# Masks in half rows, work moved to ScalarE, and half of the second attention's queries transposed in mid-step

## The chip, the core and the metric

The kernel runs on one core of a Trainium2 chip: TensorE (matmuls, with its weight loads shown as PEld), VectorE (DVE), ScalarE (ACT), GpSimd (POOL) and SyncE (SP), which start DMAs and wait for each other on semaphores. The metric is the device time of one execution in microseconds, the median of several.

## The reference

The input is 16 sequences of 256 tokens with 128 features. Layer 0 is: half a mixture of experts, attention, half a mixture; layer 1 the same with other formulas.

```python
x = x + 0.5 * _L0_ffn_ref(_layernorm(x), ...)   # top 2 of 8 experts, capacity, exact gelu, 128-512-128
x = x + _L0_attn_ref(_layernorm(x), ...)        # 16 heads of 8, rotation, distance decay, causal mask
x = x + 0.5 * _L0_ffn_ref(_layernorm(x), ...)
x = x + 0.5 * _L1_ffn_ref(_layernorm(x), ...)   # top 2 of 8 experts, silu(a) * g, biases
x = x + _L1_attn_ref(_layernorm(x), ...)        # q, k, v with bias, each head normed, no mask
x = x + 0.5 * _L1_ffn_ref(_layernorm(x), ...)
```

The attention core, for a batch b and a head h of 8 features, with all pairs of 256 queries and 256 keys:

```python
scores = einsum(q, k) / sqrt(8)                 # layer 0: + decay, -inf above the diagonal
out = softmax(scores) @ v
out = out @ Wo
```

## The kernel before

The program runs ten stages one after another, with a barrier between them: setup, token stage t0, experts e0, causal attention a0, experts e1, token stage t1, experts e2, full attention a1, experts e3, token stage t2. Tokens stay in SBUF in `x_res`. A token stage goes over 16 batches of 256 tokens: it adds the experts' gated results (`Combine`, L224), norms the rows (`Norm`, L292), chooses two experts (`Route`) and scatters each token's row twice into slots in memory, by four indirect DMAs per batch that GpSimd issues (`pool_scatter`, L545). The routed rows, with their row number as a 129th word, are written twice side by side by VectorE (`dve_rows`, L339).

An attention stage (`attention_stage`, L783) does the same around the attention, as a pipeline written out by hand: each engine has its own `causal_step(s, u)` or `full_step(s, u)`, and these lists set the order on that engine. In step s TensorE computes scores for batch s and exponent inputs for batch s-1; the combining and norm are done for batch s+3, the projection for s+2, the operands for s+1, the division, output projection and residual for s-2, and the routing for s-3.

Each batch has 16 units of two heads. `scores` (L1693) fills one of two PSUM tiles `psS`, from 54 rows of bf16 parts at partitions 0 or 64 (r = unit mod 2); VectorE takes the row maximum (`unit_max`, L1098); unit n+2 waits for the maximum of unit n. When all maxima of a batch are there, VectorE writes them, negated and split in two, into the operand `ext` (`max_rows`, L1105); TensorE transposes the queries again with them (`queries`, L1703, two halves t, into `psA` and `psD`), and VectorE and ScalarE copy the halves to `QM` (`queries_out`, L1112 and L1484). Then `e` (L1734) computes score minus maximum, transposed, in 56 rows, ScalarE takes the exponential (`unit_exp`, L1500), and `unit_v` (L1742) multiplies by the values (fp32, column tiles of 32). `weighted_out` copies the sums from PSUM: half on ScalarE (L1491), half on VectorE (L1126). In the causal stage each unit opens with a mask product of 128 rows and 256 columns, identity times mask, for scores (L1689) and for exponents (L1730).

The projection's result is copied by ScalarE with the token's norm as scale in the causal stage (L1439), and by VectorE with norm and bias in the full one (L1068). GpSimd in the full stage scales heads, takes the two rests of the bf16 splitting (`left_of_a`, `left_of_b`), scatters batch s-3, and computes both norms' reciprocal roots. `Combine.dve_gate` (L257) copies the gates of a batch, and a one-element copy (L276) marks that they were used.

## Time and profile before

| | us |
|---|---|
| median of three runs | 1839.45 (1837.21 to 1840.55) |
| profiled execution | 1845.23, its span 1843.4 |
| TensorE, weight loads busy | 1337.0 (73%), 867.6 (47%) |
| VectorE busy | 1118.2 (61%) |
| ScalarE busy | 702.6 (38%) |
| GpSimd busy | 876.2 (48%) |

Busy shares are means over ten stages that differ; matmuls overlap, so a busy TensorE is not one at its peak. a0 lies at about 250 to 690 us, a1 at about 1135 to 1645 us. In names `<-` means output from inputs, `x` a count, and what stands in brackets is how long the engine was idle before and who released it; "issue" means that nothing in the profile released it.

### The profile page before, as it was taken

To read this page: it belongs to the slowest core of one execution; us is meant where nothing else is said; L and a number is where in the kernel's file an instruction comes from. 1 tells how busy PE (TensorE), PEld (TensorE's weight loads), DVE (VectorE), ACT (ScalarE), POOL (GpSimd) and SP (SyncE) were. 2 spreads that over 40 slices of the span, in tenths; PEclk is the share of its full clock that TensorE was granted. 3 is DMA by queue.
4 is the path that set the end of the run, shared out by engine and by line. 5 is a ranking of instruction groups with operands and counts; after the bars stand their busy time and mean duration, and the time that the engine had idled before them with its cause. 6 is when DMAs were issued, how large, how long until landed. Compare 5 with 4: busy or idle time off the path is not lost. (4 is left out here: it accounts for less than half of the span.)

```text
span 1843.4 us, 34564 instructions
## 1 busy us (share of the span) xinstructions
PE 1337.0 (73%) x10630; PEld 867.6 (47%) x10630; DVE 1118.2 (61%) x4074; ACT 702.6 (38%) x1370; POOL 876.2 (48%) x1148
## 2 busy tenths in 40 slices
PE   3359938998888884994328883687878888838880
PEld 2249923444444433994216772333334334427770
DVE  6622246877887743224874444797888787644446
ACT  1112225766666641221012221475565566502220
POOL 5745535345545322554774562535454444225560
PEclk9999967999999975997559996698898787959995
DMA  9312216544000001222316672000000000026664
GB/s 286 111 48 70 71 49 152 126 99 92 22 21 13 13 13 30 73 71 76 89 44 193 198 203 78 12 13 24 18 17 20 14 12 7 14 68 190 201 181 143
DMA packets 105370, 146.31 MB, mean 79 GB/s; under 512 B 14192, under 2 KB 84336, under 8 KB 105264
## 3 DMA queue, kind: packets, MB, share of 16 engines
q1 hardware_dynamic: 85824, 107.07, 21.9%
q0 software_dynamic: 17408, 35.82, 5.7%
q10 hardware_dynamic: 2032, 2.10, 0.4%
q8 instruction: 56, 0.92, 0.2%
q14 instruction: 50, 0.41, 0.1%
HBM read 80.53 MB, written 64.40 MB: 79 GB/s over the span
## 5 line engine op out<-in xcount | busy, mean ns | idle before, releaser
L1505 ACT ACTIVATE a_PT<-a_psE 128x512 f32<-128x512 f32 (+1 forms) x512 | 273.5, 545 | 223.0 <-PE a_psE L1738 209.3
L1102 DVE TENSOR_REDUCE a_mx<-a_psS 128x2 f32<-128x512 f32 (+1 forms) x512 | 311.8, 617 | 40.6 <-PE a_psS L1697 31.4
L1697 PE MATMUL a_psS<-a_KT,a_QT 54*128 54x256 bf16 (+1 forms) x1024 | 189.6, 284 | 38.5 <-DVE a_mx L1102 34.6
L1738 PE MATMUL a_psE<-a_QM,a_KT 56*128 56x256 bf16 (+1 forms) x1024 | 194.1, 279 | 13.7 <-issue 6.6
L2166 PE MATMUL e_psH<-e_rowsT,e_w 128*128 128x256 f32 x640 | 164.4, 402 | 38.9 <-DVE e_rowsT L2206 24.8
L1762 PE MATMUL a_psV<-a_PT,a_vx 128*32 128x256 f32 (+1 forms) x2048 | 174.3, 393 | 16.4 <-ACT a_PT L1505 14.5
L2245 POOL DMA_INDIRECT slots_y<-e_y,e_ids x160 | 155.3, 970 | 46.6 <-issue 24.6
L2197 ACT ACTIVATE e_sg<-e_psH,e_w 128x256 f32<-128x256 f32 x160 | 67.1, 470 | 230.0 <-PE e_psH L2166 165.9
L2166 PEld LDWEIGHTS e_psH<-e_rowsT,e_w 128*128 128x128 f32 x640 | 120.3, 198 | 61.5 <-DVE e_rowsT L2206 25.1
L2080 POOL DMA_INDIRECT slots_y<-e_y,e_ids x128 | 124.2, 970 | 48.3 <-POOL e_ids L2078 28.8
L2044 ACT ACTIVATE e_hT<-e_psH 128x1024 f32<-128x1024 f32 x64 | 65.5, 1024 | 184.2 <-PE e_psH L2016 184.2
L2016 PE MATMUL e_psH<-e_rowsT,kept_w 128*128 128x256 f32 x512 | 128.7, 397 | 2.2 <-DVE e_rowsT L2061 2.2
L1697 PEld LDWEIGHTS a_psS<-a_KT,a_QT 54*128 54x128 bf16 x1024 | 56.4, 97 | 152.0 <-issue 69.8
L2025 PE MATMUL e_psY<-kept_w,e_hT 128*128 128x128 f32 x1024 | 124.6, 275 | 0.0
L2025 PEld LDWEIGHTS e_psY<-kept_w,e_hT 128*128 128x128 f32 x1024 | 119.6, 192 | 0.1
L2206 DVE COPY e_rowsT<-e_psT 128x256 f32<-128x256 f32 x80 | 33.9, 424 | 132.0 <-PE e_psT L2159 73.6
L2016 PEld LDWEIGHTS e_psH<-e_rowsT,kept_w 128*128 128x128 f32 x512 | 96.7, 199 | 15.3 <-DVE e_rowsT L2061 3.8
L1015 POOL TENSOR_TENSOR a_left<-a_left,a_ext 128x512 f32<-128x512 f32 x32 | 37.7, 1177 | 127.2 <-DVE a_ext L1091 127.2
L2175 PE MATMUL e_psY<-e_w,e_hT 128*128 128x128 f32 x640 | 87.6, 281 | 3.4 <-DVE e_hT L2211 3.4
L2061 DVE COPY e_rowsT<-e_psT 128x256 f32<-128x256 f32 x64 | 27.2, 425 | 102.6 <-PE e_psT L2008 102.6
L2175 PEld LDWEIGHTS e_psY<-e_w,e_hT 128*128 128x128 f32 x640 | 80.9, 198 | 3.9 <-DVE e_hT L2211 3.8
L1762 PEld LDWEIGHTS a_psV<-a_PT,a_vx 128*32 128x32 f32 x2048 | 44.6, 111 | 78.8 <-issue 40.4
(347 smaller groups left out, 2944.4 us busy)
## 6 DMA issues: line engine op xcount, KB each, us to landing
e_w<-in_pack SPq DMA_DIRECT2D x80, 450.0 KB
slots_x<-tail SPq DMA_DIRECT2D x8, 2193.0 KB
e_rows<-slots_x SPq DMA_DIRECT2D x80, 129.0 KB
e_rows<-spans_x SPq DMA_DIRECT2D x64, 129.0 KB
a_got<-slots_y SPq DMA_DIRECT2D x32, 256.0 KB
t_got<-slots_y SPq DMA_DIRECT2D x32, 256.0 KB
slots_y<-e_y,e_ids POOLq DMA_INDIRECT x288
spans_x<-tail SPq DMA_DIRECT2D x4, 1032.0 KB, 10.2
```

What stands on the lines that cost most here:

```text
L1102: nc.vector.tensor_reduce(mx[u][:, t, 4 * g + r:4 * g + r + 3:2], psS[c % 2][:, :, 0:cols], AX, ALU.max).then_inc(s_max, 1)
L1505: nc.scalar.activation(PT[:, c % 4, :, q0:SEQ], psE[c % 2][:, :, q0:SEQ], ACT.Exp).then_inc(s_e, 1)
L1697: ins = nc.tensor.matmul(psS[c % 2][:, hh, 0:cols], QT[u][64 * r:64 * r + MAXR, k, t * P:(t + 1) * P], KT[u][64 * r:64 * r + MAXR, k, 0:co ...
L1738: ins = nc.tensor.matmul(psE[c % 2][:, hh, q0:SEQ], KT[u][64 * r:64 * r + MAXR + 2, k, kt * P:(kt + 1) * P], QM[64 * r:64 * r + MAXR + 2, ...
L1762: last = nc.tensor.matmul(psV[g // 2][32 * quad:32 * quad + 32, g % 2, q0:SEQ], vx[u][:, kt, head, :], PT[:, c % 4, hh, q0:SEQ], start=(kt ...
L2016: last = nc.tensor.matmul(psH[j % 2][:, c, :], w[:, j // KEPT_TILES, c * P:(c + 1) * P], rowsT[:, j % 2, :], start=True, stop=True)
L2025: last = nc.tensor.matmul(psY[j % 2][:, s * D:(s + 1) * D], hT[:, j % 2, c, s * P:(s + 1) * P], w[:, j // KEPT_TILES, UP + c * D:UP + (c + ...
L2080: pool.indirect_dma_start(slots_out, bass.IndirectOffsetOnAxis(ap=ids[:, j % U, s:s + 1].bitcast(U32), axis=0), y[:, j % U, s, :], None).t ...
L2166: last = nc.tensor.matmul(psH[u % 2][:, c, :], w[:, u, c * P:(c + 1) * P], rowsT[:, u % 2, :], start=True, stop=True)
L2175: last = nc.tensor.matmul(psY[u % 2][:, s * D:(s + 1) * D], hT[:, u % 2, c, s * P:(s + 1) * P], w[:, u, DOWN0 + c * D:DOWN0 + (c + 1) * D] ...
L2197: ins = nc.scalar.activation(sg[:, u % 2, c, :], psH[u % 2][:, c, :], ACT.Silu, bias=w[:, u, B1 + c:B1 + c + 1])
L2245: pool.indirect_dma_start(slots_out, bass.IndirectOffsetOnAxis(ap=ids[:, u, s:s + 1].bitcast(U32), axis=0), y[:, u, s, :], None).then_inc( ...
```

## The change

- Masks: each 128-row mask product becomes two of 64 rows (`scores_mask`, `e_mask`), in the row half that the unit's data uses; the first covers 256 columns, the second only the 128 in which its rows mask anything. They are issued alternately for the two units in work.
- ScalarE takes over: the second half of the weighted values (at the start of the next step); in the full stage both projection copies (the norm's scale is put on the tokens before they are transposed, the bias comes from an added product of a constant matrix with the bias), and the routed rows as x * rstd + shift, shift computed by GpSimd; the gates' copy; in the other stages the second copy of the routed rows. The marker copy becomes a bare semaphore increment.
- `QM` has two buffers, and `max_rows` runs once per half. In the full stage the first half of the queries is transposed at n == 9 of the batch's own step and copied after maximum 11; operands come one unit earlier; the scatter is of batch s-4 and stands between the two rests; VectorE's list is reordered.

```diff
+    def act_gate(self, act, b, u):
+
+        wait(act, self.s_added, b - 1)
+        self.nc.scalar.copy(self.gate[:, u, :].rearrange("p (t k) -> p t k", t=TPB),
+                            self.keep.gates[:, bass.ds(b * TPB, TPB), :]).then_inc(self.s_gate, 1)
...
-            nc.vector.tensor_copy(self.used[:, u:u + 1], self.gate[:, u, 0:1]).then_inc(self.s_added, 1)
+            dve.sem_inc(self.s_added, 1)
...
+            if self.to_scatter:
+                nc.vector.tensor_scalar(self.less[:, u, :], self.mv[:, u, :, 0], -1.0, None,
+                                        ALU.mult).then_inc(self.s_less, 1)
...
-            self.out[:, w, t, :, 0:D], x.to_broadcast([P, TOPK, D]),
+            self.out[:, w, t, 0, 0:D].unsqueeze(1), self.keep.x[:, bass.ds(b * TPB + t, 1), :],
...
+    def act_second(self, act, b, w):
...
+        self.nc.scalar.copy(self.out[:, w, :, 1, 0:D], self.out[:, w, :, 0, 0:D]).then_inc(self.s_second, 1)
...
+        self.nc.gpsimd.tensor_tensor(self.shift[:, u, :], self.less[:, u, :], self.rstd[:, u, :],
+                                     ALU.mult).then_inc(self.s_shift, 1)
...
+    def act_rows(self, act, b, u, w):
+
+        act.wait_ge(self.s_shift, b + 1)
+        act.wait_ge(self.s_ids, b + 1)
+        for t in range(TPB):
+            ins = self.nc.scalar.activation(
+                self.out[:, w, t, :, 0:D], self.keep.x[:, bass.ds(b * TPB + t, 1), :].to_broadcast([P, TOPK, D]),
+                ACT.Identity, scale=self.rstd[:, u, t:t + 1], bias=self.shift[:, u, t:t + 1])
+        ins.then_inc(self.s_out, 1)
...
+        wait(pool, self.norm.s_out if by_act else self.norm.s_second, b + 1)
...
+                if has(s - 4):
+                    route.pool_scatter(pool, chain, s - 4, u, True)
                 if has(s + 1):
                     left_of_b(s + 1, v)
-                if has(s - 3):
-                    route.pool_scatter(pool, chain, s - 3, v)
...
+                    route.norm.pool_shift(pool, s - 2, u)
...
+            if not causal:
+                route.pool_scatter(pool, chain, BATCHES - 1, 1, True)
...
-                dst = [ext[u][:, :, 0, :, MAXR + n] for n in range(2)]
-                link(nc.vector.tensor_scalar(dst[0], mx[u][:, :, :], -1.0, None, ALU.mult))
-                nc.vector.scalar_tensor_tensor(out=dst[1], in0=mx[u][:, :, :], scalar=-1.0,
+            def max_rows(b, u, t):
+                dve.wait_ge(s_max, UNITS * b + 8 * (t + 1))
+                dst = [ext[u][:, t, 0, :, MAXR + n] for n in range(2)]
...
+                wait(dve, s_E, UNITS * (b - 1))
+                nc.vector.tensor_copy(QM[u][:, :, 0:P].bitcast(U32),
                                       psA[:, :].bitcast(U32).rearrange("p (k q) -> p k q", k=8)).then_inc(s_QM[0], 1)
...
-                rows(0)
+                if has(s + 3):
+                    dve.wait_ge(comb.s_gate, s + 4)
+                add(0, 0)
                 maxima(1, 2)
-                rows(1)
+                add(0, 1)
                 maxima(2, 3)
                 if has(s - 2):
                     divide(s - 2, 0)
+                add(1, 0)
                 maxima(3, 4)
-                if has(s + 3):
-                    comb.dve_gate(dve, link, s + 3, v)
-                add(0, 0)
-                maxima(4, 5)
                 if has(s + 1):
                     split_a(s + 1, v)
+                maxima(4, 5)
+                add(1, 1)
+                maxima(5, 6)
                 if has(s - 2):
                     divide(s - 2, 1)
-                maxima(5, 6)
-                add(0, 1)
-                add(1, 0)
+                do(stats, 0)
                 maxima(6, 7)
-                if has(s + 2):
-                    project_out(s + 2, u, 0)
+                if has(s + 1):
+                    split_b(s + 1, v)
+                do(stats, 1)
                 maxima(7, 8)
                 for n in range(5):
                     do(choose, n)
+                    do(stats, n + 2)
                 maxima(8, 9)
-                if has(s + 1):
-                    split_b(s + 1, v)
-                add(1, 1)
+                if has(s):
+                    max_rows(s, u, 0)
                 maxima(9, 10)
-                if has(s + 2):
-                    project_out(s + 2, u, 1)
                 do(number, 0)
                 do(number, 1)
                 maxima(10, 11)
-                if has(s - 2):
-                    route.dve_ids(dve, s - 2, u)
+                if has(s + 1):
+                    split_c(s + 1, v)
                 do(number, 2)
                 maxima(11, 12)
+                if has(s):
+                    queries_out(s, u)
                 do(number, 3)
-                if has(s + 1):
-                    split_c(s + 1, v)
-                do(number, 4)
+                if has(s + 2):
+                    head_var(s + 2, u)
                 maxima(12, 13)
                 if has(s - 2):
                     residual(s - 2)
+                do(number, 4)
                 maxima(13, 14)
                 if has(s - 2):
-                    link.sync()
-                    dve.sem_inc(s_xr, 1)
-                do(stats, 0)
-                if has(s + 2):
-                    head_var(s + 2, u)
-                do(stats, 1)
+                    route_stats(s - 2, u)
...
+                    max_rows(s, u, 1)
                 if has(s + 1):
                     last_operand_out(s + 1, v)
-                if has(s):
-                    queries_out(s)
-                if has(s - 1):
-                    weighted_out(s - 1, v)
                 link.restart()
             step = causal_step if causal else full_step
...
+            def scaled_tokens_out(b, u):
+                act.wait_ge(norm.s_rstd, b + 1)
+                wait(act, s_xaT_ps, b - 1)
+                for t in range(TPB):
+                    ins = nc.scalar.activation(xs[:, u, t, :].unsqueeze(1), keep.x[:, bass.ds(b * TPB + t, 1), :],
+                                               ACT.Identity, scale=norm.rstd[:, u, t:t + 1])
+                ins.then_inc(s_xs, 1)
...
+            def scaled_project_out(b, u, t):
+                act.wait_ge(s_proj, TPB * b + t + 1)
+                if t == 0:
+                    wait(act, s_v, b - 1)
+                nc.scalar.copy(pr[:, u, t, :], psA[:, 0:QKV]).then_inc(s_pr, 1)
...
+            def weighted_out(b, u, n):
+
+                act.wait_ge(s_V, UNITS * b + 8 * (n + 1))
+                nc.scalar.copy(oT[u][:, 2 * n:2 * n + 2, :], psV[n][:, :, :]).then_inc(s_oT[n], 1)
...
+                exps(0, 1)
+                if has(s - 3):
+                    route.norm.act_rows(act, s - 3, v, v)
+                exps(1, 2)
                 if has(s + 2):
                     tiles_out(s + 2)
-                exps(3, 5)
+                exps(2, 4)
                 if has(s - 3):
                     route.act_T(act, s - 3, v, psT)
+                exps(4, 5)
+                if has(s + 2):
+                    scaled_project_out(s + 2, u, 0)
                 exps(5, 6)
-                exps(6, 7)
                 if has(s + 1):
                     copies_of_a(s + 1, v)
-                exps(7, 8)
+                exps(6, 8)
+                if has(s + 2):
+                    scaled_project_out(s + 2, u, 1)
                 if has(s - 2):
                     divided_out(s - 2)
                 exps(8, 9)
+                if has(s + 1):
+                    copies_of_b(s + 1, v)
                 exps(9, 10)
                 if has(s - 1):
-                    weighted_out(s - 1, v)
-                if has(s + 1):
-                    copies_of_b(s + 1, v)
-                exps(10, 11)
+                    weighted_out(s - 1, v, 0)
                 if has(s + 2):
                     squares(s + 2, u)
+                exps(10, 11)
+                if has(s + 3):
+                    scaled_tokens_out(s + 3, v)
                 exps(11, 12)
-                if has(s + 3):
-                    tokens_out(s + 3, v)
-                exps(12, 14)
+                if has(s + 4):
+                    comb.act_gate(act, s + 4, u)
+                exps(12, 13)
                 if has(s + 1):
                     operands_out(s + 1, v, 0)
-                exps(14, 15)
+                if has(s + 2):
+                    heads_log(s + 2)
+                exps(13, 14)
+                if has(s + 2):
+                    heads_rsqrt(s + 2)
                 if has(s + 1):
                     operands_out(s + 1, v, 1)
-                if has(s + 2):
-                    heads_log(s + 2)
-                exps(15, 16)
-                if has(s + 2):
-                    heads_rsqrt(s + 2)
+                exps(14, 16)
                 if has(s + 1):
                     operands_out(s + 1, v, 2)
...
+                if not causal:
+                    nc.tensor.matmul(psA[:, 0:QKV], mean_of[:, :], par[:, BI0:BI0 + QKV],
+                                     start=True, stop=False, skip_group_check=True)
                 nc.tensor.matmul(psA[:, 0:QKV], xaT[:, t * P:(t + 1) * P], wqkv[:, :],
-                                 start=True, stop=True).then_inc(s_proj, 1)
+                                 start=causal, stop=True, skip_group_check=True).then_inc(s_proj, 1)
...
-                    nc.tensor.matmul(psS[c % 2][:, :, t * P:(t + 1) * P], identb[:, :],
-                                     masks[:, 0, :].unsqueeze(1).to_broadcast([P, 2, P]), start=True, stop=False,
-                                     skip_group_check=True)
+                    scores_mask(c, 0)
+
+            def scores_mask(c, i):
+
+                t, g, r = unit_b(c)
+                rows, lo = slice(64 * r, 64 * r + 64), 64 * i
+                nc.tensor.matmul(psS[c % 2][:, :, t * P + lo:(t + 1) * P], half_ident[rows, i, :],
+                                 masks[rows, 0, i, lo:P].unsqueeze(1).to_broadcast([64, 2, P - lo]),
+                                 start=(i == 0), stop=False, skip_group_check=True)
             def scores(u, c, hh):
                 t, g, r = unit_b(c)
...
+                rows, hi = slice(64 * r, 64 * r + 64), 64 * (i + 1)
+                nc.tensor.matmul(psE[c % 2][:, :, kt * P:kt * P + hi], half_ident[rows, i, :],
+                                 masks[rows, 1, i, 0:hi].unsqueeze(1).to_broadcast([64, 2, hi]),
+                                 start=(i == 1), stop=False, skip_group_check=True)
...
+                    if has(s) and n < UNITS - 2:
+                        scores_mask(n + 2, 1)
+                    if has(s - 1) and n < UNITS - 1:
+                        e_mask(n + 1, 0)
                     for hh in range(2):
...
-                    queries(s - 1, v, 0)
...
+                    if n == 9 and has(s):
+                        queries(s, u, 0)
...
+                    if n == 11 and has(s + 1):
+                        operands(s + 1, v, 0)
                     if n == 12 and has(s + 1):
-                        operands(s + 1, v, 0)
+                        operands(s + 1, v, 1)
                     if n == 13 and has(s + 1):
-                        operands(s + 1, v, 1)
-                    if n == 14 and has(s + 1):
                         operands(s + 1, v, 2)
                 if has(s + 1):
...
+    half = P // 2
+    twice = [np.tile(m[i * half:(i + 1) * half], (2, 1)) for m in (above * MASKED, above.T * MASKED, np.eye(P))
+             for i in range(2)]
+    return np.concatenate([ang, pos] + twice, 1).astype(np.float32)
```

## Rows read from the trace of the kernel before

**Rows 1.** Busy by stretch: length, PE (x), PEld, DVE, ACT, POOL, granted clock, DMA share, GB/s.
```profile
308.20:665.00 356.80, 319.65 (x3509) 161.97 (x3510) 275.94 (x941) 229.75 (x490) 159.42 (x197) 0.99 0.24 56
1188.40:1599.20 410.80, 339.27 (x3058) 158.02 (x3059) 331.66 (x956) 249.83 (x488) 183.37 (x231) 0.85 0.05 16
```

**Rows 2.** One line (VectorE's query copies): duration min/median/max, first and last start.
```profile
L1116 DVE COPY a_QM<-a_psA x16: 680/692/693, 308.2 to 665.0; 128x512 uint32<-128x512 uint32 x16
...
L1116 DVE COPY a_QM<-a_psA x16: 681/691/693, 1188.4 to 1599.2; 128x512 uint32<-128x512 uint32 x16
```

**Rows 3.** Waits, TensorE's loads, 308.2 to 665: us in total, times, longest.
```profile
PEld a_psS L1697 <- issue: 44.3, 207, 0.4
PEld a_psS L1689 <- DVE a_mx L1102: 21.4, 51, 1.0
```

**Rows 4.** Timeline, first attention, one unit: start, duration, instruction [idle before it].
```profile
442.00 0.28 PE L1689 MATMUL a_psS<-a_masks,a_identb 128*128 128x256 bf16 x1
...
442.12 0.27 PE L1730 MATMUL a_psE<-a_masks,a_identb 128*128 128x256 bf16 x1
...
442.32 0.28 PE L1697 MATMUL a_psS<-a_KT,a_QT 54*128 54x256 bf16 x1
442.32 0.28 PE L1738 MATMUL a_psE<-a_QM,a_KT 56*128 56x256 bf16 x1
...
442.64 0.43 PE L1762 MATMUL a_psV<-a_PT,a_vx 128*32 128x128 f32 x8
```

**Rows 5.** Waits, second attention, 1188.4 to 1599.2, of three engines.
```profile
PEld a_psS L1697 <- DVE a_mx L1102: 49.8, 75, 1.4
...
DVE a_QM L1116 <- PE a_psA L1720: 30.7, 15, 3.2
...
ACT a_PT L1505 <- PE a_psE L1738: 101.4, 115, 2.8
```

**Rows 6.** Timeline of VectorE, second attention, a step's end.
```profile
1311.79 0.69 DVE L1102 TENSOR_REDUCE a_mx<-a_psS 128x2 f32<-128x512 f32 x1
...
1316.38 0.69 DVE L1116 COPY a_QM<-a_psA 128x512 uint32<-128x512 uint32 x1 [1.98 <-PE a_psA L1720]
...
1317.59 0.68 DVE L1102 TENSOR_REDUCE a_mx<-a_psS 128x2 f32<-128x512 f32 x1
```

**Rows 7.** VectorE's groups, second attention, last row first attention: busy us, mean ns | idle.
```profile
L1073 DVE SCALAR_TENSOR_TENSOR a_pr<-a_psA,a_attn_rstd,a_par 128x384 f32<-128x384 f32 x26 | 15.9, 613 | 5.1 <-PE a_psA L1642 4.8
L344 DVE TENSOR_SCALAR a_route_out<-x_res,a_route_mv,a_route_rstd 128x256 f32 x16 | 15.9, 995 | 0.0
...
L344 DVE TENSOR_SCALAR a_route_out<-x_res,a_route_mv,a_route_rstd 128x256 f32<-128x256 f32 x10 | 8.0, 803 | 0.0
...
L276 DVE COPY a_used<-a_gate_b 128x1 f32<-128x1 f32 x12 | 1.8, 154 | 0.4
...
L344 DVE TENSOR_SCALAR a_route_out<-x_res,a_route_mv,a_route_rstd 128x256 f32 x16 | 5.8, 409 | 0.0
```

**Rows 8.** ScalarE's groups: from the first attention, then from the second.
```profile
L1442 ACT ACTIVATE a_pr<-a_psA,a_attn_rstd 128x384 f32<-128x384 f32 x26 | 15.1, 580 | 6.0 <-PE a_psA L1642 4.5
...
L1494 ACT COPY a_oT<-a_psV 128x512 f32<-128x512 f32 x15 | 8.8, 585 | 0.0
```

**Rows 9.** Page, section 5, a ScalarE group with a bias from memory.
```profile
L2197 ACT ACTIVATE e_sg<-e_psH,e_w 128x256 f32<-128x256 f32 x160 | 67.1, 470 | 230.0 <-PE e_psH L2166 165.9
```

**Rows 10.** Timeline, second attention: projections in its steady part, and at its start.
```profile
1297.88 0.91 PE L1642 MATMUL a_psA<-a_wqkv,a_xaT 128*128 128x384 f32 x2
...
1145.49 1.65 PE L1642 MATMUL a_psA<-a_wqkv,a_xaT 128*128 128x384 f32 x2 [0.46 <-ACT a_xaT L1434]
```

**Rows 11.** Timeline of GpSimd, second attention: the first residue, and a scatter.
```profile
1296.08 1.16 POOL L1011 TENSOR_TENSOR a_left<-a_qk,a_ext 128x512 f32<-128x512 f32 x1 [2.90 <-DVE a_ext L1087]
...
1311.39 0.96 POOL L551 DMA_INDIRECT slots_x<-a_route_out,a_rows  x1 [0.30 <-issue]
```

**Rows 12.** Timeline of GpSimd, second token stage.
```profile
923.31 0.22 POOL L549 TENSOR_TENSOR t_rows<-t_rows,no_rows 128x4 int32<-128x4 int32 x1 [0.24 <-DVE t_rows L539]
```

150 lines of the change are left out of this document (81 added, 69 removed).

## Prediction

> **What bounds the kernel now.** I read the busy times by stretch first [rows 1]. The two attention stages take most of the span: their steady parts are 356.8 and 410.8 us, each 15 steps long (from the first to the last of 16 copies of one kind [rows 2]), so a step takes 23.8 us in the first attention and 27.4 us in the second. Per step VectorE is busy 275.94/15 = 18.4 us and 331.66/15 = 22.1 us, ScalarE 15.3 and 16.7 us. No engine is full; each step is a chain of 16 units, handed from TensorE (scores) to VectorE (row maximum) and, one batch behind, from TensorE to ScalarE (exponential) and back, and TensorE issues all of it in one order. So I read next who waits for whom.
>
> In the **first attention** [rows 3] TensorE's mask loads wait 21.4 us in all for maxima (1.4 a step), but its score loads show 44.3 us with "issue" as the reason, 207 pieces of about 0.2 us: there it waits for nobody, the array is finishing. One unit in close order [rows 4] shows what that is: the mask product for scores starts at 442.00, the one for the exponentials at 442.12, the data products only at 442.32, the next work at 442.64. Same shape follows same shape after 0.12 us; from a 128-row mask to 54- or 56-row data takes 0.20 us, and the two rounds of data leave the same 0.32 = 0.12 + 0.20 us until the next shape. TensorE paces the middle of this step, VectorE comes close behind.
>
> In the **second attention** [rows 5] there are no masks. TensorE's score loads wait 49.8 us for maxima (3.3 us a step); VectorE's largest wait is 30.7 us (2.05 a step) for the transposed queries at the end of the step. VectorE paces the middle, and between the last maximum of a step (ends 1312.48) and the first of the next (1317.59) lie 5.1 us [rows 6]: two maximum rows, a copy of keys, 1.98 us of waiting for the transposed queries, their copy (0.69), the copy of weighted values. The granted clock is 0.99 in the first and 0.85 in the second stage [rows 1]; 0.85 is a mix of the two levels, 2.4 GHz for 70% of the time and 1.2 GHz for 30%.
>
> **The change, part by part.** *Masks.* The 128-row product of 256 columns becomes two 64-row products of 256 and 128 columns, in the rows of the array which its unit uses; the other unit's mask has the other rows. The trace shows data products of the two units starting within 0.01 us of each other [rows 4], but no 64-row mask. If the halves overlap likewise, a unit runs 0.12 + 0.06 (128 columns, half of 0.12), then data at once: data starts 0.18 instead of 0.32 us after the mask, 0.14 saved, and 0.08 more where the next unit follows without another shape between. If they do not overlap, 0.12 + 0.12 + 0.06 + 0.06 = 0.36 us, 0.04 lost. Bounds -0.04 and +0.22; I take 0.17 a unit, since the data products do overlap: 15 x 0.17 = 2.6 us of TensorE a step. A page of the Trainium skill, TensorE: Matmul & The Clock Gate (Part 3, Measured speedup vs the span model), has four row tiles gaining 3.07 times instead of 4. Scaled that way my 0.18 would be 0.23 us, by an estimate from that page 0.8 us a step and 12 us of the total less; no row here shows packed masks.
>
> *VectorE, second attention* [rows 7], per step: both projection outputs go (15.9/13 = 1.22), both routed-row writes ((15.9 + 8.0)/13 = 1.84), the copy of weighted values (0.69, as the copy of the same size [rows 6]), gate copy and the marker copy behind it (0.15 for the marker, 0.2 taken for the gates). Sum 4.1. Added: the maximum rows are done in two halves (two operations more, each at least as long as the marker's 0.154 [rows 7]; between 0.3 and 0.55, I take 0.4) and one small negation, 0.17. Net -3.5: 22.1 becomes 18.6.
>
> *ScalarE, second attention.* Two projection copies of 384 columns: 0.585 is the price of 512 columns, 0.58 that of 384 with a scale from memory [rows 8], so less than both, I take 0.48 and 0.1 for a scale: 2 x 0.48; weighted values 0.585; tokens scaled in two pieces instead of one copy, about +0.33; routed rows 2 x 0.47 to 0.57 (nearest: 128x256 with a bias, 0.47 [rows 9]), 1.05; gates about 0.2 (bounds 0.15 to 0.4). Together +3.1: 16.7 becomes 19.8. The first attention gets weighted values, the second copy of routed rows (half the columns of the weighted values, 0.4) and gates: +1.2, to 16.5. These have cover: ScalarE idles 101.4/15 = 6.8 us a step before exponentials in the second attention [rows 5]. Queued behind each new wait (shifts and row numbers, scaled tokens behind the norm of GpSimd) are the next exponentials, then the weighted-value products on TensorE.
>
> The Trainium skill, ScalarE: Activation LUTs (Rules for kernel authors), speaks against this half: it sends additions and multiplications to VectorE, not ScalarE. The rows say otherwise here: the same routed-row operation takes 0.41 us in the first attention, but 0.995 and 0.80 us in the second, beside GpSimd's long operations [rows 7]. At 0.41 the move would relieve VectorE by 0.82 instead of 1.84 a step, 16 us less in all.
>
> *TensorE, second attention.* The bias now comes from a product with the array, twice a step. A projection took 0.91 us at the high and 1.65 at the low level [rows 10]; the difference, 0.74, is its column time at 2.4 GHz, so +1.5 us a step. It has no product to hide under but takes time in which TensorE waits for maxima (3.3 a step).
>
> *The turn of the step.* Half of the queries move to unit 9, and their copy to unit 11, so the 1.98 us wait and two copies of 0.7 leave the gap. What is late next: key copy on ScalarE, other half of the queries, first scores. I put VectorE's idle time at 27.4 - 22.1 = 5.3 today, minus 2.05, plus 1.0 for those scores, plus 1.8 for ScalarE and the bias product coming into the pace: 6.1. Step: 18.6 + 6.1 = 24.7, **2.7 us less, x 16 = 43 us**.
>
> *First attention.* VectorE loses the copy of weighted values (0.69), gate and marker (0.3), about 0.3 of the routed rows (written once instead of twice, two operations of 0.41 [rows 7]), gains 0.6: -0.7. TensorE loses 2.6, so VectorE's idle 23.8 - 18.4 = 5.4 falls by half of that, 1.3 (the other half runs into VectorE's own load). 23.8 - 0.7 - 1.3 = 21.8, **2.0 less, x 16 = 32 us**. The queries still turn at the step's end there. Double buffering QM costs nothing.
>
> *Moved past queues.* In the second attention GpSimd now scatters one batch later, but ahead of the second residue and the norm; four scatters at 0.96 with 0.30 in front of each, and 0.5 for the numbers ahead of them, are 5.5 us [rows 11]. Today the first residue ends at 1297.24; with the scatters behind it the second would start at 1302.8, as today, and the norm end near 1304.8 (two operations, 1.16 and 0.7), while ScalarE's scaled tokens come up near 1305: no cost, but little to spare.
>
> *The rest.* The first token stage is paced by GpSimd (its four scatters [rows 11] fill the step); ScalarE's added copy comes a batch earlier: 0. In the second, GpSimd waits 0.24 us a step for VectorE's row numbers [rows 12]: at most 16 x 0.24 = 4, I take 3; last stage 1. At the start of the second attention, at 1.2 GHz, two bias products (1.5 each) and the norm ahead of the token copy (about 2) lie bare: +5, less 2 at its end, where the last norm no longer stands behind four scatters: +3.
>
> **Sum.** -43 - 32 - 4 + 3 = -76 us. The profiled execution took 1845.2 us (span 1843.4), 5.8 above the median of 1839.45; taken from the median: **1763 us**.
>
> **The rivals.** (A) *Masks pay nothing*: the halves follow each other. For it: no 64-row mask in the trace. Against: the data pairs. The first attention then keeps its pace: 1763 + 32 = 1795. (B) *The pace follows VectorE's load fully*: the turn and the clock recover (clock near 1.0, idle 3.3 instead of 6.1 in the second, another 1.3 in the first): 2.8 x 16 + 1.3 x 16 = 66 less, 1697. For it: long waits at the turn coincide with clock 0.85. Against: three engines near 19 to 21 us in a 24 us step. (C) *Slower: ScalarE's idle time is not slack*. Each idle stretch before an exponential is the latency of the loop exponential, TensorE, exponential; work put in it delays TensorE's one queue, and with it the scores. Then the second attention's step grows by the 3.1 us and gains nothing, the first is only 2.0 - 1.2 = 0.8 shorter: 16 x 3.1 - 16 x 0.8 = +37, 1876; it turns slower once 76/16 = 4.75 us a step more than I counted is lost in the second stage, or half as much in both. For it: 6.8 us a step in waits for products [rows 5]. Against: VectorE is what TensorE waits for longest.
>
> **Chances.** Forecast (1735 to 1785) 0.62; A 0.16; B 0.12; C, in full or enough of it, 0.08; about unchanged 0.02. The range takes in A with its bound (masks 0.6 us a step worse, 1805, and the doubled costs of the gate and row operations, 10 more) and half of the way to B: 1712 to 1815. A measurement of this kernel can tell about 0.2% from no change. Faster 0.90, same 0.02, slower 0.08.
>
> **What would show it.** In the first attention: masks of both units starting together and data 0.2 us after them; a 21 to 22 us step. In the second: no VectorE wait of 2 us at the query copy, VectorE busy 18 to 19 us, ScalarE 19 to 20, a step near 24.7. Wrong: ScalarE waiting at the scaled tokens or shifts, with TensorE waiting for exponentials; masks one after another; or steps shorter than 23.

## The result, and the profile after

The kernel after takes 1813.76 us in the median (1808.81 to 1817.36, 4 runs), the kernel before beside it 1838.33 (1829.92 to 1840.55, 4 runs): ratio 0.9864, interval 0.9824 to 0.9904. So it is faster by 25 us, where 76 were forecast; the forecast of 1763 lies 51 us below, and the range (1712 to 1815) holds the time by one microsecond. Its profiled execution took 1808.81 us, with a span of 1807.0 (before 1843.4). The two profiled executions lie 36 us apart and the medians 25; what follows places the 36.

All this is one chip. Chips differ here by more than the change is worth, which only the experiments showed, each group of them on one chip: the kernel before took 1741 us on chip 7, 1742 on chip 14, 1743 on chip 3, 1745 and 1741 on chip 4, and 1842 on chip 8, like the first chip. I call the first chip and number 8 the slow kind, the others the quick kind.

The same two stretches as in [rows 1], of the kernel after (busy time of TensorE, its weight loads, VectorE, ScalarE and GpSimd, then the granted clock); again 15 steps each, from the first to the last copy of the queries:

```profile
307.40:663.10 355.70, 300.04 (x3987) 179.10 (x3987) 266.49 (x947) 238.51 (x527) 159.37 (x197) 0.98 0.23 56
1175.20:1553.90 378.70, 315.39 (x3095) 158.47 (x3099) 317.72 (x902) 281.15 (x577) 181.31 (x239) 0.92 0.05 16
```

A step of the **first attention** takes 355.7/15 = 23.71 us (before 23.79): no gain at all, though TensorE's busy time fell by 19.6 us. A step of the **second** takes 378.7/15 = 25.25 us (before 27.39): 2.14 less, 34 us over 16 steps. The copy of the queries stands some 8 us earlier in its step now, which moves both of its marks alike. The 36.4 us by which the span is shorter are these 34 and 2 elsewhere.

In a single unit the masks do what was forecast. One unit in the first attention's middle, TensorE (start, duration, line), to be held against [rows 4]:

```profile
431.73 0.28 PE L1755 MATMUL a_psS<-a_masks,a_half_ident 64*128 64x256 bf16 x1
431.74 0.28 PE L1803 MATMUL a_psE<-a_masks,a_half_ident 64*128 64x256 bf16 x1
431.85 0.22 PE L1755 MATMUL a_psS<-a_masks,a_half_ident 64*128 64x128 bf16 x1
...
431.91 0.27 PE L1763 MATMUL a_psS<-a_KT,a_QT 54*128 54x256 bf16 x1
...
432.22 0.32 PE L1835 MATMUL a_psV<-a_PT,a_vx 128*32 128x128 f32 x4
```

Both masks start at 431.73, data 0.18 us behind, the next work at 0.49 instead of 0.64. But the waits of the stage, against [rows 3] (total us, times, longest):

```profile
PEld a_psS L1755 <- DVE a_mx L1135: 42.8, 87, 1.3
...
DVE a_mx L1135 <- PE a_psS L1763: 20.2, 27, 1.9
```

TensorE's loads now wait 42.8 us for maxima, before 21.4: what the masks gave up became waiting. Over a step TensorE's busy time fell by 1.3 us (19.6/15), half of the 2.6 that 0.17 us a unit had promised. In the second attention VectorE's wait at the query copy (30.7 us, [rows 5]) is gone, but VectorE's busy time fell only to 317.72/15 = 21.2 us a step, where 18.6 was forecast. Its groups there (busy us, mean ns), to be held against the 349 and 425 ns that an addition took before (L268 there):

```profile
L274 DVE SCALAR_TENSOR_TENSOR x_res<-a_got,a_gate_b,x_res 128x128 f32 x32 | 25.3, 791 | 0.0
...
L274 DVE SCALAR_TENSOR_TENSOR x_res<-a_got,a_gate_b,x_res 128x128 f32<-128x128 f32 x16 | 11.2, 699 | 0.0
...
L1142 DVE SCALAR_TENSOR_TENSOR a_ext<-a_mx,a_ext 128x16 bf16<-128x16 f32 x30 | 10.5, 349 | 1.0
...
L1141 DVE TENSOR_SCALAR a_ext<-a_mx 128x16 bf16<-128x16 f32 x30 | 7.4, 248 | 0.5
L336 DVE TENSOR_SCALAR a_attn_vare<-a_attn_mv 128x2 f32<-128x2 f32 x12 | 7.3, 610 | 0.3
```

An addition takes 791 and 699 ns, and a variance of two numbers a partition 610. The timeline of one step's start, VectorE and GpSimd, shows where:

```profile
1387.79 1.25 DVE L274 SCALAR_TENSOR_TENSOR x_res<-a_got,a_gate_b,x_res 128x128 f32 x1
...
1389.57 0.87 DVE L274 SCALAR_TENSOR_TENSOR x_res<-a_got,a_gate_b,x_res 128x128 f32 x1
...
1387.63 1.27 POOL L1031 TENSOR_TENSOR a_pt<-a_pt,a_par 128x512 f32<-128x512 f32 x1
1389.03 1.27 POOL L1035 TENSOR_TENSOR a_qk<-a_pt,a_par 128x512 f32<-128x512 f32 x1
...
1391.45 0.34 DVE L274 SCALAR_TENSOR_TENSOR x_res<-a_got,a_gate_b,x_res 128x128 f32 x1
...
1398.96 1.57 DVE L336 TENSOR_SCALAR a_attn_vare<-a_attn_mv 128x2 f32<-128x2 f32 x1
...
1399.33 1.16 POOL L1055 TENSOR_TENSOR a_left<-a_left,a_ext 128x512 f32<-128x512 f32 x1
```

Beside GpSimd's products of 512 columns an addition takes 1.25 and 0.87 us, the next one, with GpSimd idle, 0.34; the variance ends just when GpSimd's second residue does. The routed rows had paid this price in that place ([rows 7]); that the additions pay it now because they took the place is what two experiments test (b_adds_late, c_rows_back).

### The profile page after: what moved, and what is told of

Same layout as the page of the kernel before. It is cut to its first block and busy times, and to the rows that moved or that the text cites. A ratio compares the mean times of both kernels' runs of the same rounds, so it can differ in the third digit from the quotient of the medians.

```text
span 1807.0 us, 36015 instructions
## 1 busy us (share of the span) xinstructions
PE 1291.6 (71%) x11206; PEld 885.7 (49%) x11206; DVE 1079.8 (60%) x4011; ACT 757.1 (42%) x1558; POOL 878.6 (49%) x1164
## 5 line engine op out<-in xcount | busy, mean ns | idle before, releaser
L1763 PE MATMUL a_psS<-a_KT,a_QT 54*128 54x256 bf16 (+1 forms) x1024 | 179.2, 270 | 51.7 <-DVE a_mx L1135 37.8
L1811 PE MATMUL a_psE<-a_QM,a_KT 56*128 56x256 bf16 (+1 forms) x1024 | 180.2, 268 | 15.4 <-issue 9.4
L1835 PE MATMUL a_psV<-a_PT,a_vx 128*32 128x256 f32 (+1 forms) x2048 | 164.8, 385 | 4.0 <-ACT a_PT L1545 3.9
L2161 POOL DMA_INDIRECT slots_y<-e_y,e_ids x128 | 124.3, 971 | 48.6 <-POOL e_ids L2159 29.1
L1763 PEld LDWEIGHTS a_psS<-a_KT,a_QT 54*128 54x128 bf16 x1024 | 65.7, 97 | 112.1 <-DVE a_mx L1135 53.7
L2287 DVE COPY e_rowsT<-e_psT 128x256 f32<-128x256 f32 x80 | 33.9, 424 | 130.1 <-PE e_psT L2240 77.2
L1755 PE MATMUL a_psS<-a_masks,a_half_ident 64*128 64x128 bf16 (+1 forms) x512 | 83.0, 252 | 30.5 <-DVE a_mx L1135 22.4
L347 POOL TENSOR_TENSOR a_route_rstd<-a_route_vare,neg_half 128x2 f32<-128x2 f32 x32 | 22.8, 714 | 149.6 <-DVE a_route_vare L336 149.2
L1803 PE MATMUL a_psE<-a_masks,a_half_ident 64*128 64x256 bf16 (+1 forms) x512 | 82.9, 250 | 14.3 <-ACT a_PT L1545 9.0
L274 DVE SCALAR_TENSOR_TENSOR x_res<-a_got,a_gate_b,x_res 128x128 f32<-128x128 f32 (+1 forms) x128 | 74.4, 581 | 24.6 <-DMA a_got<-slots_y 22.6
```

What stands on the lines that cost most here:

```text
L274: ins = nc.vector.scalar_tensor_tensor(out=keep.x[:, bass.ds(b * TPB + t, 1), :], in0=self.got[:, w, t * TOPK + k, :].unsqueeze(1), scalar ...
L1763: ins = nc.tensor.matmul(psS[c % 2][:, hh, 0:cols], QT[u][64 * r:64 * r + MAXR, k, t * P:(t + 1) * P], KT[u][64 * r:64 * r + MAXR, k, 0:co ...
L1811: ins = nc.tensor.matmul(psE[c % 2][:, hh, q0:SEQ], KT[u][64 * r:64 * r + MAXR + 2, k, kt * P:(kt + 1) * P], QM[u][64 * r:64 * r + MAXR + ...
L1835: last = nc.tensor.matmul(psV[g // 2][32 * quad:32 * quad + 32, g % 2, q0:SEQ], vx[u][:, kt, head, :], PT[:, c % 4, hh, q0:SEQ], start=(kt ...
L2161: pool.indirect_dma_start(slots_out, bass.IndirectOffsetOnAxis(ap=ids[:, j % U, s:s + 1].bitcast(U32), axis=0), y[:, j % U, s, :], None).t ...
```

## The experiments

Theories at the start: **1**, the first attention is paced by the turns that VectorE and TensorE give each other at fixed places of their lists; **2**, in the second attention VectorE's relief was eaten by operations set beside GpSimd's long ones. Rivals: TensorE's amount of work, or ScalarE's. A third theory came with the second group.

### Masks, and the order of VectorE's lists (chip 7)

a_masks_whole:
```diff
-  half_ident[rows, i, :], masks[rows, 0, i, lo:P]   (two 64-row products a unit and kind)
+  identb[:, :], mask_w[:, 0, :]                     (one 128-row product)
```


> The kernel after, with the causal masks of the first attention written as whole 128-row products again (two per unit instead of four of 64 rows); all else as after. Theory 1 (order): the first attention is paced by the turns that VectorE and TensorE give each other at fixed places of their lists, and the TensorE time of the masks lies in TensorE's waits, which went from 21.4 to 42.8 us on the maxima: a step of 23.7 to 24.0 us, the whole kernel 0 to 5 us slower than after. Rival (TensorE's throughput, the prediction's own term): a step of 25.5 to 26 us, the kernel 28 to 35 us slower than after.

a_masks_none: the scores_mask and e_mask calls removed, data products with start=True.

> The kernel after with the causal mask products of the first attention left out (64 matmuls a step and 5 to 8 us of TensorE's time in 23.7); queries then see later keys, so this part of the computation is changed. Theory 1: a step within 1 us of 23.7, the kernel 0 to 16 us faster than after. Rival (TensorE's throughput): a step of 20 us or less, the kernel 50 us or more faster.

a_list_first, VectorE's list (M is a maximum, C the choice, N the numbers, S the norm's statistics, rows the maximum rows, stats the statistics of the residual):
```diff
-  add(1,1) C0 split_b C1 M5 C2 ... M7 S1 N0 S2 M8 rows N1 M9 N2 split_c N3 M10 M11 M12 residual stats M13
+  add(1,1) split_b M5 C0 C1 C2 ... M7 S1 M8 N0 S2 rows N1 M9 split_c N2 M10 M11 M12 N3 residual M13 stats
```


> The kernel after with VectorE's list of the first attention reordered, no work changed: the row maximum of unit 5 ahead of the logits that it waited 1.0 us for, that of unit 8 ahead of the prefix counts (0.5), that of unit 13 ahead of the statistics of the residual (1.2), and two route operations later. Theory 1: VectorE's waits shrink and with them TensorE's on the maxima, a step of 22.0 to 23.2 us, the kernel 8 to 27 us faster than after. Rival (both engines limited by their amount of work, or by the wait near unit 14 that the list does not touch): a step of 23.5 to 23.8, the kernel within 3 us of after.

a_list_second:
```diff
-  M7 C0 S2 C1 C2 C3 C4 M8 rows M9 N0 N1 M10
+  M7 M8 C0 C1 C2 C3 C4 rows M9 N0 N1 S2 M10
```


> The kernel after with VectorE's list of the second attention reordered, no work changed: the maximum of unit 8 ahead of the choice of experts, behind which TensorE waited up to 2.65 us, and the variance with its epsilon (610 ns a piece, 1567 at most, beside GpSimd's left-overs) taken out of the choice, behind the numbers. Theory 2 (the place of small operations beside GpSimd's long ones, and the choice as one block, cost what the prediction counted as won): a step of 23.8 to 24.8 us instead of 25.25, the kernel 7 to 23 us faster than after. Rival (ScalarE, with its 3 us a step more, is now what paces it): a step of 25.0 to 25.4, the kernel within 4 us of after.

Measured against before: 1.0025 [0.9996, 1.0053], 1.0063 [1.0030, 1.0096], 1.0015 [0.9985, 1.0045] and 0.9989 [0.9953, 1.0025]. The kernel after was not timed on this chip; a_list_first and a_list_second each share one attention with it. Nothing was clearly faster than before here, whose median was 1741.12. The steady parts of the first attention, 15 steps, of a_masks_whole, a_masks_none, a_list_first and a_list_second (in the last this attention is that of after):

```profile
311.30:657.10 345.80, 312.90 (x3509) 162.19 (x3508) 273.55 (x947) 245.84 (x527) 159.45 (x197) 1.00 0.23 58
```
```profile
305.40:659.80 354.40, 292.83 (x3027) 153.66 (x3025) 276.29 (x946) 238.02 (x527) 159.49 (x197) 0.82 0.23 56
```
```profile
308.00:645.00 337.00, 300.20 (x3984) 181.63 (x3981) 278.62 (x947) 239.69 (x527) 157.10 (x195) 0.94 0.24 59
```
```profile
306.50:649.70 343.20, 294.74 (x3990) 178.26 (x3991) 274.94 (x948) 241.78 (x528) 159.34 (x197) 0.97 0.24 58
```

Held against the last, whole masks cost TensorE 18.2 us of busy time and the stage 2.6: 0.17 us a step, where the forecast had 1.3 (2.0 with VectorE's own relief). Masks left out altogether don't help either: the step is 23.63 us, and the granted clock falls from 0.97 to 0.82, a mix with 1.2 GHz for a third of the time. What TensorE doesn't do, it waits: its loads wait 29.4 us for maxima with whole masks, 46.9 with halved ones, 43.2 with none. Both readings speak against TensorE's amount, but not cleanly: the clock was 1.00 with whole masks, 0.97 with halved ones and 0.82 with none, so each saving met a lower clock. The test that leaves the work alone comes with d_best. The first list took the step from 22.88 to 22.47, in the direction of theory 1 but at the weak end. The second took the variance from 446 ns (a_masks_whole, same list as after) to 168, and the step from 24.65 to 24.53 only, where at least 0.45 was forecast; on chip 14 the same list (in b_lists_both) went from 24.77 to 24.03. The granted clock fell in the first pair (0.92 to 0.91) and rose in the second (0.92 to 0.94), so the list's own worth stays between the two.

### Both kernels on one quick chip, and the additions moved (chip 14)

b_before and b_after are unchanged; b_lists_both has both lists above. b_adds_late, second attention:
```diff
-  M0 add(0,0) M1 add(0,1) M2 divide add(1,0) M3 split_a M4 add(1,1) M5 divide S0 M6 split_b S1 M7 C0 S2 ...
+  M0 M1 M2 divide M3 split_a M4 M5 divide add(0,0) add(0,1) M6 split_b add(1,0) add(1,1) M7 M8 C0 ... S0 M9 S1 N0 N1 S2
```


> The kernel after, unchanged, timed side by side with the kernel before on one chip. The first measurement gave 0.9864 of the time before. On the chip of the first four runs the stages around the attentions were shorter (the mid part 487 to 494 us instead of 512) and before took 1741 us. If the gain is in the second attention's step alone (theory 2) and belongs to the kernels, it is 20 to 34 us on any chip, ratio 0.980 to 0.988. If it was made larger by the chip's clock in the step's turn (before: 0.85 granted in that stage), it is smaller where before keeps its clock: ratio 0.992 to 1.000.

> The kernel before, unchanged, for a profile from the same chip as the others. Expected by theory 1 a first-attention step equal to that of after within 0.3 us; by theory 2 a second-attention step 2 us longer than after's. If the gain depends on the chip, the second-attention step of before is here 25 to 26 us and its granted clock over 0.90.

> The kernel after with both reordered VectorE lists (those of a_list_first and a_list_second). The first brought its attention's step from 22.9 to 22.5 us and the second from 24.65 to 24.5: if the parts add up, 8 us faster than after; if TensorE's granted clock answers (0.94 instead of 0.97 in the first attention's stage with the list), 0 to 3 us.

> The kernel after, second attention only: the four combining additions moved from behind maxima 0 to 4, where GpSimd's scaling of the heads runs (1.07 and 1.27 us an instruction), to behind maxima 5 and 6, with the statistics later and the maximum of unit 8 ahead of the choice. Theory 2 (the additions pay for GpSimd's long instructions): an addition takes 350 to 450 ns instead of 650 to 860, VectorE's busy time falls by 1.2 to 1.6 us a step, and the step from 24.6 to 23.3 to 24.0 us, the kernel 10 to 20 us faster than after. Rival (GpSimd's hold falls on whatever VectorE does there, or TensorE is the pace): the additions get shorter but the step stays within 0.3 us of 24.6.

Ratios to before: after **1.0036 [1.0008, 1.0063]**, lists_both 0.9977 [0.9949, 1.0005], adds_late 0.9867 [0.9820, 0.9915]; b_before, the same kernel against itself, 1.0009 [0.9970, 1.0047]. So on a quick chip the change gains nothing; it loses a little. From the first attention's steady part to the end, in four stretches, b_before and then b_after:

```profile
307.20:656.60 349.40, 317.88 (x3508) 162.64 (x3506) 279.38 (x941) 232.98 (x489) 159.48 (x197) 0.98 0.24 57
656.60:1149.10 492.50, 327.70 (x2037) 268.25 (x2035) 254.42 (x1045) 104.51 (x191) 266.13 (x359) 0.77 0.34 100
1149.10:1526.10 377.00, 328.88 (x3057) 154.71 (x3057) 325.56 (x955) 248.58 (x487) 182.48 (x230) 0.87 0.06 17
1526.10:1745.80 219.70, 141.32 (x888) 116.87 (x885) 119.20 (x407) 47.03 (x105) 99.43 (x137) 0.82 0.57 164
```
```profile
310.20:652.40 342.20, 293.35 (x3989) 178.60 (x3987) 275.36 (x946) 241.55 (x527) 159.38 (x197) 0.97 0.25 59
652.40:1149.30 496.90, 337.18 (x2025) 272.89 (x2023) 242.60 (x1023) 112.19 (x222) 264.92 (x356) 0.75 0.34 99
1149.30:1520.90 371.60, 315.41 (x3101) 158.33 (x3100) 322.05 (x901) 280.02 (x577) 181.29 (x239) 0.92 0.05 16
1520.90:1750.90 230.00, 151.91 (x941) 120.71 (x933) 118.25 (x403) 54.14 (x118) 104.65 (x146) 0.79 0.55 158
```

The steps are shorter by 7.2 and 5.4 us in all (23.29 to 22.81 and 25.13 to 24.77 us each), the rest is longer by 17.7: 3.0 ahead of these stretches, where nothing was to change, 4.4 between the attentions and 10.3 behind. The last is no accident: that stretch is 228 to 233 us in every whole kernel of the quick chips with the change's second attention, 219.7 before. About 8 us of it are the query copy's earlier place in its step, the rest (0 to 5) is not traced. The other parts are within the spread of single executions. GpSimd's last scatters of the first attention (duration, first and last start) look like a cost of the change, 39.5 us behind the last steady step before and 45.4 now:

```profile
L551 POOL DMA_INDIRECT spans_x<-a_route_out,a_rows x24: 954/958/1129, 602.7 to 696.1; - x24
```
```profile
L588 POOL DMA_INDIRECT spans_x<-a_route_out,a_rows x24: 954/958/1057, 600.9 to 697.8; - x24
```

But b_adds_late has the same first attention on the same chip and takes 39.2 us there, a_masks_whole 39.5, and on the first chip the change shortened it from 48.6 to 44.8. So no cost of the draining steps is shown.

The additions in b_adds_late:

```profile
L274 DVE SCALAR_TENSOR_TENSOR x_res<-a_got,a_gate_b,x_res 128x128 f32 x32 | 15.5, 483 | 1.7 <-DVE x_res L274 1.4
...
L274 DVE SCALAR_TENSOR_TENSOR x_res<-a_got,a_gate_b,x_res 128x128 f32<-128x128 f32 x16 | 7.9, 494 | 0.4 <-issue 0.2
```

483 and 494 ns instead of 763 and 650; VectorE's busy time in the stage 306.9 instead of 322.1, 1.0 us a step, and the step 24.12 instead of 24.77. Theory 2 is confirmed in kind: the additions got shorter where they were put. All its sizes were off (350 to 450 ns, 1.2 to 1.6 us of VectorE and a step of 23.3 to 24.0 were forecast). The whole kernel gained 26 us on after, more than the 10 to 20 forecast and more than 16 times 0.65; its profiled execution took 1734.73, 13 us over its median, so this trace is not a typical one.

What made the step of *before* 27.4 us on the first chip and 25.1 here? The turn of one step in the first trace of before, TensorE and ScalarE, with the first of GpSimd's four scatters of that step (the last begins at 1311.39):

```profile
1307.50 1.06 POOL L551 DMA_INDIRECT slots_x<-a_route_out,a_rows  x1 [0.29 <-POOL a_rows L549]
...
1308.51 0.62 PE L1676 MATMUL a_psV<-a_identb,a_ext 128*128 128x128 bf16 x8
...
1312.10 0.51 PE L1676 MATMUL a_psV<-a_identb,a_ext 128*128 128x128 bf16 x6 [0.65 <-ACT a_QT L1481]
1313.26 0.27 PE L1676 MATMUL a_psV<-a_identb,a_ext 128*128 128x128 bf16 x2 [0.65 <-issue]
...
1315.09 0.63 PE L1762 MATMUL a_psV<-a_PT,a_vx 128*32 128x256 f32 x4 [1.00 <-ACT a_PT L1505]
...
1311.03 1.01 ACT L1481 COPY a_QT<-a_psV 128x1024 bf16<-128x1024 bf16 x1 [2.09 <-PE a_psA L1676]
```

and the same place on chip 14, where the scatters begin at 1260.61:

```profile
1263.20 0.62 PE L1676 MATMUL a_psV<-a_identb,a_ext 128*128 128x128 bf16 x8
...
1265.97 0.61 PE L1676 MATMUL a_psV<-a_identb,a_ext 128*128 128x128 bf16 x8
1266.51 1.10 PE L1762 MATMUL a_psV<-a_PT,a_vx 128*32 128x256 f32 x8
...
1263.86 1.01 ACT L1481 COPY a_QT<-a_psV 128x1024 bf16<-128x1024 bf16 x1 [0.28 <-PE a_psV L1676]
```

On the first chip TensorE stops in the middle of eight transposes between which there is no wait in the program, and again within eight weighted-value products, where the program does wait for ScalarE's exponential. I call a pause of 0.3 us or more within such a run a break. Over 15 steps I count 23 breaks with 18.7 us in that stage, 9 of them (5.3 us) at places without a wait, and 1 in the first attention. In the kernel after there are none in the second attention but 13 (6.1 us) in the first. On chip 14 neither kernel has one. They come 4 to 8 us behind the first of the batch's four scatters.

The breaks are only the visible part. ScalarE's copy of the first eight transposes needs nothing but their signal; it starts 1.90 us after they end (1308.51 + 0.62), on chip 14 0.04. So I held the time of each signal of TensorE that the trace records against the end that it gives the product. In the steady parts of both attentions some 930 signals each are recorded. On the slow kind 79 to 111 of them come more than 0.4 us late, up to 4.1, all between 1.3 and 6.2 us behind the first scatter of a batch, in every trace of both kernels and of the kernels below (before 79 and 87, after 96 and 89). In the 14 traces of quick chips not one does. The ends of products are modelled in the trace, but the engines that waited did start with the late signals.

**Theory 3**: on the slow kind, the traffic of the scatters holds up TensorE, and a kernel loses or wins by what stands there. The change did not take this away from the second attention (87 late signals before, 89 after); it moved the scatters from the turn to the middle of the step, past maxima for which TensorE waits anyway, and the breaks at the turn went. Whether the supply of instructions is held up, or their completion, the traces don't say. Nor are the two kinds set apart by this alone: between the first chip and chip 14 the kernel before differs by 7 and 34 us in the attentions, and by 31 and 24.5 us in the stretches between and behind them, so most of what makes a chip slow lies elsewhere.

### One part undone at a time (chip 8, slow kind)

These four are set against the kernel after, which itself was not timed on chip 8. c_best: the first list of a_list_first and the second of b_adds_late. c_queries_back: the queries' first half at the turn again:
```diff
+  queries(s - 1, v, 0)
   queries(s - 1, v, 1)
...
-  if n == 9 and has(s):
-      queries(s, u, 0)
```
c_no_bias: the product with mean_of and the bias removed. c_rows_back: act_rows off ScalarE; M0 rows(0) add(0,0) M1 rows(1) add(0,1) on VectorE (rows(t) are routed rows here).

> The kernel after with VectorE's list of the first attention as in a_list_first and that of the second as in b_adds_late. Each alone gave a step 0.2 to 0.4 us shorter (first) and 0.65 us shorter (second) than after's 22.8 and 24.8. If they add up: 13 to 20 us faster than after, ratio to the kernel before 0.98 to 0.99 where after itself is at 1.00. Rival (TensorE's clock gives way as its work gets denser): no better than b_adds_late's 1721 us.

> The kernel after with both halves of the second attention's queries transposed at the start of the step again, the first of them copied by VectorE at the end of its list (one part of the change undone). The prediction valued the wait that goes at 1.98 us a step; on the chip of b_before that wait was 0.4 us a step only, and there were no breaks inside TensorE's runs of eight transposes, of which the first chip's trace of the kernel before had 23 with 18 us in this stage. If those breaks made the wait: on a chip without them this kernel is 5 to 16 us slower than after (0.3 to 1.0 us a step), on one with them 25 us or more. Rival (the wait belongs to the order): 25 to 35 us slower on any chip.

> The kernel after with the bias products of the second attention's projection left out (two a batch, about 0.65 us each at full clock, 1.3 us of TensorE's time a step; the projection's bias is then missing from the result). Rival (TensorE's throughput paces the stage): 1.0 to 1.5 us a step, 16 to 24 us faster. Theory 2 (VectorE's list and its turns with TensorE pace it): at most 0.4 us a step, 0 to 6 us faster.

> The kernel after with the routed rows of the second attention computed by VectorE again, two of 128x256 behind the first two maxima, and the additions right behind them; ScalarE is spared 1.2 us a step. Theory 2 (what stands first in VectorE's list while GpSimd scales the heads pays for it, and what comes later does not): rows at 700 to 1000 ns instead of the 400 of a quiet moment, the additions at 350 to 550 ns instead of 650 to 760, VectorE's busy time up by 1 us a step and not by 1.8, the step 0 to 0.8 us longer. Rival (each operation has its own price): rows 800 ns, additions unchanged, VectorE up by 1.6 us or more and the step with it.

Ratios to before (1842.32 here): 0.9928 [0.9897, 0.9959], 0.9873 [0.9827, 0.9919], 0.9822 [0.9774, 0.9869], 0.9864 [0.9816, 0.9912]. The second attention's steps are 24.86, 25.66, 25.09 and 26.05 us; after's own 25.25 comes from the first chip, of the same kind (in the three kernels whose first attention is that of after, its step here is 23.6 to 23.7, there 23.71). The granted clocks of that stage are 0.93, 0.89, 0.89 and 0.90, after's 0.92; as the last group shows, such a difference alone can move a step by several tenths of a microsecond, so the step times of single traces here are weaker evidence than the waits and the durations. By whole times, after (0.9864 on the first chip), queries_back and rows_back can't be told apart.

*Queries back*: +0.4 us a step. VectorE waits 8.5 us in all for the transposed queries, 0.57 a step and not 1.98, and there are no breaks at the turn. So the wait that the prediction cashed in was mostly not the price of the order: with the scatters elsewhere, the old order waits about a quarter as long. *Bias left out*: -0.16 a step for 1.3 us less of TensorE's work, at a lower clock (0.89 instead of 0.92), so how much of it the amount is worth at one clock stays open. *Rows back*, VectorE's groups:

```profile
L274 DVE SCALAR_TENSOR_TENSOR x_res<-a_got,a_gate_b,x_res 128x128 f32 x32 | 18.1, 565 | 0.0
L369 DVE TENSOR_SCALAR a_route_out<-x_res,a_route_mv,a_route_rstd 128x256 f32 x16 | 16.6, 1040 | 0.0
...
L274 DVE SCALAR_TENSOR_TENSOR x_res<-a_got,a_gate_b,x_res 128x128 f32<-128x128 f32 x16 | 9.2, 578 | 0.0
L369 DVE TENSOR_SCALAR a_route_out<-x_res,a_route_mv,a_route_rstd 128x256 f32<-128x256 f32 x10 | 9.2, 921 | 0.0
```

Rows at 1040 and 921 ns, and the additions behind them down from 791 and 699 to 565 and 578: the place pays, whoever stands in it. VectorE's total grew by 10 us (0.7 a step, theory 2 had 1) and the step by 0.8, the upper end of theory 2. *c_best* was a surprise: its second attention is fast, but its first takes 24.42 us a step, slower than before, though the same list had 22.5 and 22.7 on the quick chips 7 and 14 (a_list_first, b_lists_both). GpSimd's first scatter of a step, and TensorE, with two breaks inside runs of eight transposes:

```profile
438.69 1.06 POOL L588 DMA_INDIRECT spans_x<-a_route_out,a_rows  x1 [0.50 <-POOL a_rows L586]
...
443.02 0.22 PE L1740 MATMUL a_psD<-a_identb,a_ext 128*128 128x128 bf16 x1 [0.34 <-issue]
...
444.49 0.44 PE L1740 MATMUL a_psV<-a_identb,a_ext 128*128 128x128 bf16 x5 [0.81 <-issue]
```

32 breaks, 22.4 us, and 111 late signals. The later row numbers had moved the scatter towards the step's end; my reading is that the breaks now fall on operands that everything waits for. With four placements of the scatters on the slow kind (the two attentions of before, the first of after, this one) TensorE's breaks begin 6.0, 4.2 to 8.0, 5.3 to 8.1 and 2.1 to 6.7 us behind the batch's first scatter: they follow the scatters.

### Without the scatters, and a better order (chips 4 and 3)

d_before_quiet, e_before_quiet and d_after_quiet:
```diff
-  pool.indirect_dma_start(...)   (four a batch, second attention)
+  pool.sem_inc(self.s_scat[w], 16 * TPB * TOPK)
...
-  expert_stage(nc, keep, "e3", slots_x, slots_y, a["pack1"])
```
d_best and f_best (the same kernel twice): second attention as in b_adds_late; first attention:
```diff
-  M5 C0 C1 C2 ... M8 N0 S2 rows N1 M9 split_c N2 M10 M11 M12 N3 residual M13 stats
+  M5 C0 C1 C2 ... M8 N0 S2 rows N1 N2 N3 M9 split_c M10 M11 M12 residual M13 stats
```
e_best2: d_best with TensorE's routed_tiles in the first attention from ahead of e_open(0) to n == 0.

> The kernel before with the second attention's scatters left out (four a batch, GpSimd writes 512 rows to memory with them), and the expert stage behind it left out too, since nothing is there for it to read; the result and the whole time are therefore not comparable, only the second attention's steady step is (27.39 us with the scatters in the first trace, 25.13 on chip 14). Theory 3 (the scatters' traffic holds up TensorE's own supply on some chips): on a chip of the slow kind no break inside a run of eight transposes, and a step of 24.8 to 25.4; on one of the fast kind a step unchanged within 0.3 us. Rival (the long step belongs to the chip in another way, memory or clock): on a slow chip the step stays at 27 or more and the breaks stay.

> The kernel after with the same left out. In its first trace TensorE stood 2.65 us at 5.0 us behind the first scatter in every second step, ahead of the choice of experts. Theory 3: on a slow chip the step goes from 25.25 to 24.0 to 24.8 us; on a fast one 24.77 stays within 0.5 us (GpSimd is also spared 5 us a step). Rival: 25.0 to 25.4 on a slow chip.

> The kernel after with the second attention's list of b_adds_late and, in the first attention, the list of a_list_first but the row numbers as early as in after, so that the scatter does not move. On chip 8 the later row numbers made the first attention's step 24.42 us instead of 23.6, with 31 breaks (21 us) in TensorE's runs. Theory 3: the breaks are back at 13 to 16 and a step of 23.0 to 23.6 on a slow chip, 22.4 to 22.8 on a fast one; with the second attention's 0.4 to 0.6 us a step the kernel is 10 to 18 us faster than after on either. Rival (the denser list itself makes the breaks): a step of 24 us or more on a slow chip.

> The kernel before with the second attention's scatters and the expert stage behind it left out, as in d_before_quiet (24.95 us a step on chip 4, of the fast kind, where 25.1 is the step with them). Theory 3 (the scatters hold up TensorE's supply): on a chip of the slow kind no break inside a run of eight transposes in the second attention and a step of 24.8 to 25.6 instead of 27.39; in the first attention, where the scatters are still there, 23.6 to 23.9 as before. Rival (another trait of the chip): a step of 26.5 or more with breaks. On a fast chip 24.8 to 25.2, which tells nothing apart.

> The kernel d_best with one more change, TensorE's transposes of the routed tiles in the first attention behind the scores of unit 2 and not ahead of the first of the second group, where TensorE waited 1.2 us a step for VectorE's rows (d_best, chip 4). By the turns that TensorE and VectorE give each other: 0.4 to 1.0 us off a step of 21.35, the kernel 6 to 16 us faster than d_best's 0.9735 of before on a fast chip, 0.965 to 0.970; on a slow one 0.970 to 0.985. Rival (that wait is hidden, since the scores it holds back wait for maxima anyway): a step of 21.2 to 21.5.

> The kernel d_best again, with more rounds. If the second attention has two modes of its own (23.6 us a step with the clock granted in full, 25.7 with 0.87), the times of one chip fall in two groups some 30 us apart: near 1702 and near 1735 on a fast chip. On a slow chip: theory 3 expects 13 to 16 breaks in the first attention as in after, a step of 22.2 to 23.2 there, 24.2 to 25 in the second, ratio 0.97 to 0.98; the rival (a denser list brings breaks of its own) 24 us or more in the first attention and a ratio of 0.985 to 0.995, as c_best had.

The quiet kernels fell on a quick chip all three times: steps of 24.95 and 24.85 us (before, 25.13 with scatters) and 24.25 (after, 24.77). That says that scatters cost the order of before at most 0.3 us a step on the quick kind, and that of after 0.5; what they do on the slow kind these runs can't tell. **Theory 3 stays open**: TensorE's late signals behind the scatters are seen in every trace of the slow kind and in none of the quick, but no run without scatters was had there, nor one that shows what the stop is made of. The kernels with the better order fell on quick chips too: what they do on the slow kind, where c_best lost in the first attention, is not measured.

d_best is 0.9735 [0.9685, 0.9784] of before (1702.19 us), f_best 0.9795 [0.9761, 0.9828] (1703.42 us, 1694.86 to 1717.11), e_best2 0.9860 [0.9758, 0.9961] (1729.77). The first attention of d_best, and the second of f_best, d_best and e_best2, where the list is the same:

```profile
309.00:629.20 320.20, 285.72 (x3985) 174.33 (x3985) 276.17 (x948) 238.77 (x528) 159.88 (x197) 1.00 0.26 63
1117.40:1471.40 354.00, 302.23 (x3099) 153.49 (x3099) 303.71 (x902) 279.50 (x579) 181.14 (x239) 0.95 0.06 17
```
```profile
1115.00:1463.40 348.40, 295.70 (x3095) 151.55 (x3099) 303.78 (x902) 278.90 (x579) 181.13 (x239) 0.98 0.06 18
```
```profile
1111.00:1497.10 386.10, 329.64 (x3095) 162.65 (x3099) 310.32 (x901) 282.25 (x579) 181.04 (x239) 0.88 0.05 16
```

In the first attention the step fell from 22.8 to 21.35 us, with no operation less: VectorE's wait for the logits from 16.4 us (b_after) to 0.7, TensorE's load waits for maxima from 47.0 to 23.7. The same list takes 21.40 on chip 3 (f_best). This is theory 1's clean test, with a gain eight times that of the masks; the clock rose too, from 0.97 to 1.00, and shares in it. e_best2's one move gave 21.15, near its rival's 21.2 and far from the 0.4 us expected at least.

The second attention of e_best2 took 25.74 us a step with a granted clock of 0.88, against 23.60 with 0.95 and 23.23 with 0.98, by the same list on chips of the same kind. Step by step, d_best's clock is 1.00 in ten steps on end; e_best2's is 0.87 in nine of its fifteen. One step of each:

```profile
1188.20:1211.80 23.60, 19.86 (x213) 10.29 (x212) 20.77 (x67) 19.12 (x42) 13.62 (x18) 1.00 0.09 24
```
```profile
1214.00:1239.70 25.70, 22.29 (x201) 10.90 (x201) 20.00 (x64) 18.74 (x40) 13.64 (x18) 0.87 0.07 22
```

So a step of this stage has two lengths with one list: 23.6 us at 2.4 GHz throughout, and 25.7 with 1.2 GHz for a quarter of it. The single times on chip 4 show it: d_best 1701.41, 1702.97, 1700.30 and once 1738.31, e_best2 1730.06, 1733.54, 1729.48 and once 1705.03, clocks of 0.880 to 0.884 in the short ones and 0.863 to 0.868 in the long. The difference between e_best2 and d_best is therefore the clock's and not the move's. The two groups some 30 us apart that f_best was to show on chip 3 did not come: its six times run from 1694.86 to 1717.11 without a gap of that size. Whether a waiting TensorE lowers the clock, or a lower clock makes the others wait, no run here separates.

This reaches back to the groups above. b_adds_late has this list too: its 24.12 at a clock of 0.94 lies between 25.74 at 0.88 and 23.60 at 0.95. Its 0.65 us on after (24.77 at 0.92) can therefore be the clock's in part; what stands without the clock is the shorter additions, VectorE's 1.0 us a step, and the ratios of several executions.

## Why the prediction was right and wrong

By the spans, 40 of the forecast 76 us did not come: 31 in the first attention (1 us gained of 32) and 9 in the second (34 of 43).

*Masks*: in one unit the size was right (0.17 us forecast, 0.15 seen, with data 0.18 us behind the mask), its worth was not. The Trainium skill (TensorE: Matmul & The Clock Gate, Part 3, Measured speedup vs the span model) has a factor for four row tiles that would have made the 0.18 0.23; the trace doesn't show it for two halves. The step that failed is "falls by half of that, 1.3" for VectorE's idle time, together with reading "issue" gaps as TensorE pacing the middle. Those gaps are real but lie between two turns with VectorE; shorter ones make the wait for the next maximum longer. Halving was worth 0.17 us a step (chip 7), not 1.3; the whole first attention gained 0.08 on the first chip and 0.48 on chip 14, not 2.0. VectorE's busy time did fall by 0.63 us a step there (0.7 forecast), and its idle time grew by nearly as much: neither engine's amount sets this step, their order does, as d_best shows (22.8 to 21.35 with the same work). Rival A gave 1795 for exactly this outcome, for a different reason (halves one after another), and was underweighted.

*VectorE, second attention*: what was removed was priced rightly per batch; what failed is that the additions kept their old 349 and 425 ns. The sum named the contention itself (0.41 against 0.995 us for the same rows) and took it for a trait of the routed rows. It belongs to the place: 36.5 us of additions in 12 batches instead of 18.0 is 1.5 us a batch, the variance 0.44, the halved maximum rows 0.6 a step instead of 0.4. There is a slip in the sum besides: its terms are per batch (divided by 13), but 22.1 and the result are means over 15 steps, in which what was removed comes to 54.0 us or 3.6 a step, not 4.1. Net -0.9, not -3.5. The Trainium skill's rule that additions and multiplications go to VectorE (ScalarE: Activation LUTs, Rules for kernel authors) would, by the prediction, have taken 16 us off the 43; the 34 that came lie between. The trace agrees with the rule where VectorE is undisturbed (0.41 us for the rows there, 0.59 on ScalarE), but the relief was lost another way: of the 1.84 us a batch taken off, 1.5 came back in the additions.

*ScalarE*: 281.15/15 = 18.7 us, 19.8 forecast; rows 590 ns each (0.52 taken), scaled tokens 408 and 433 (0.37), projection copies 477 (0.48). No wait at the scaled tokens or the shifts in the steady steps of after, on either chip (b_adds_late and c_best have 1.4 and 1.8 us in all): rival C did not come.

*The turn*: that "the 1.98 us wait and two copies of 0.7 leave the gap" came true on the first chip, and is most of its gain. But it was mostly a wait for a TensorE held up behind the scatters, not for the order of the transposes: 0.4 us a step in b_before, 0.57 in c_queries_back. Right number, wrong mechanism; on the quick kind there was nothing to gain, and the forecast of faster with 0.90 is refuted there (1.0036).

*Idle time at the turn*: 6.1 a step was forecast, 4.1 was seen (378.7 - 317.7 over 15), so the step of 24.7 against 25.25 looks better than its terms were: VectorE 2.6 us more, idle 2.0 less.

*GpSimd's scatters ahead of the second residue*: "no cost, but little to spare" held for the norm. What no step counted is where their traffic falls. *The edges*: +3 forecast; the end of the second attention is longer by 0 to 5 us on the quick chips, where 2 less were counted, and the rest can't be told from the spread. *The range*: "half of the way to B" is 1730, not 1712; the bound that mattered was the other one.

## What to carry to other kernels

In a list-ordered pipeline with two buffers between two engines, work taken from one of them pays only where its partner isn't behind another fixed turn: moving maxima ahead of operations that wait gave 1.4 us a step (22.8 and 22.9 on chips 14 and 7, 21.35 on chip 4), halving TensorE's mask products 0.17. Where GpSimd runs long products, price a place in VectorE's list and not an operation, since the next one put there takes over the slowness. And a gain read from one chip's trace is that chip's: look whether the wait that is to go contains breaks inside runs without waits, or signals that come later than the work that they tell of, and at the granted clock step by step, before it is booked. The same holds for the test afterwards: two single traces whose clocks differ by 0.02 do not price a reordering of half a microsecond.

## What the runs showed of the hardware

- Chips of one type differ by 5 to 6% on the same program (1741 to 1745 against 1838 to 1842 us). On the slow kind about a tenth of TensorE's signals in the attentions (79 to 111 of some 930) come 0.4 to 4.1 us late, all within 1.3 to 6.2 us behind the first of four scatters of 128 rows, and TensorE pauses inside runs of independent products; on the quick kind none does. Cause open.
- Less work went with a lower clock: without the masks the first attention's granted clock was 0.82 instead of 0.97, and the step 0.75 us longer than with them.
- One list on one chip had a stage at 0.95 of the clock or at 0.88, with 2.1 us a step between them.
- A 128x2 operation of VectorE on SBUF took 1.57 us beside a GpSimd operation of 512 columns and 163 ns elsewhere; the row maxima from PSUM kept their 685 ns throughout (682 before).
